# A first unit's projections in an order of their own, six gate tiles ahead of the convolution tiles, and a wider pad ahead of the scan's buffers

## The reference

```python
proj = input_states @ in_proj_w.T
gate, xBC, dt = proj[..., :8192], proj[..., 8192:18432], proj[..., 18432:]
xBC = silu(causal_conv4(xBC) + conv_b)
hs, Bm, Cm = xBC (128 heads of 64), 8 groups of 128, 8 groups of 128
dt = softplus(dt + dt_bias);  A = -exp(A_log);  cum = cumsum(dt * A)
y = scan over the sequence(hs, A, Bm, Cm, D, dt)
g = group_rms_norm(y * silu(gate)) * norm_w
x = x + g @ out_w.T                      # input_states = layernorm(x)
x = x + ffn(layernorm(x))                # ffn(x) = lin2(silu(lin1(x)) * lin3(x))
```

## Time and profile before

| | |
|---|---|
| median of 3 runs | 1926.45 us (1924.99 to 1927.78) |
| profiled execution, its own time | 1926.12 us |
| span in its profile | 1924.3 us |
| PE busy | 1817.4 us, 94% of the span |
| DVE busy | 1204.2 us, 63% |
| ACT busy | 1143.8 us, 59% |
| POOL busy | 1066.4 us, 55% |

### The profile page before, as it was taken

The page is one execution under the profiler, slowest core; times in us unless marked ns, Lnnn a source line. Parts: engine busy times, 40 slices in busy tenths (PEclk is TensorE's granted clock), DMA queues, the critical chain, the costliest instruction groups (busy, mean ns, idle before and its releaser), DMA issues.

```text
span 1924.3 us, 27364 instructions
## 1 busy us (share of the span) xinstructions
PE 1817.4 (94%) x9826; PEld 1448.3 (75%) x9826; DVE 1204.2 (63%) x2070; ACT 1143.8 (59%) x2185; POOL 1066.4 (55%) x989
## 2 busy tenths in 40 slices
PE   5879999999999999999999999999999997689999
PEld 3668777778777877787778777787777785467767
DVE  5456667766776768666867686668667776613112
ACT  4666667666766676666766676667666764322111
POOL 3346666666656566665756575757565654432121
PEclk9989999999999999999999999999999998889989
DMA  3523334333433343334433353335333522221001
GB/s 121 152 90 116 107 116 151 115 103 116 151 110 109 107 144 104 121 89 140 125 105 119 116 147 107 115 105 163 106 113 104 157 86 69 73 71 37 28 21 44
DMA packets 118709, 205.36 MB, mean 107 GB/s; under 512 B 23888, under 2 KB 28368, under 8 KB 118576
## 3 DMA queue, kind: packets, MB, share of 16 engines
q1 hardware_dynamic: 118576, 203.62, 34.8%
HBM read 198.85 MB, written 4.72 MB: 106 GB/s over the span
## 4 chain that ended last, share of the span: by engine, by line
PE 80%; DVE 10%; POOL 5%; ACT 2%; issue 2%; DMA 1%; SPq 0%; DVEq 0%; POOLq 0%; ACTq 0%
PE bank L1280 15%; PE bank L1282 14%; PE bank L1281 14%; PE bank L1343 6%; PE bank L1381 5%; PE bank L1356 5%; PE bank L1383 4%; PE bank L1382 4%; PE bank L1369 3%; PE bank L1321 3%; DVE ow_l L1074 2%; DVE x_ch L1068 2%; DVE bcT L1068 2%; POOL xw L614 1%; DVE xdt L1087 1%
## 5 line engine op out<-in xcount | busy, mean ns | idle before, releaser
L596 POOL TENSOR_TENSOR w_l<-w_raw,w_h 128x512 fp32r<-128x512 f32 x288 | 373.0, 1298 | 315.1 <-ACT w_h L726 313.7
L1280 PE MATMUL bank<-x_h,w_h 128*128 128x512 f32 x1160 | 473.5, 408 | 24.3 <-DVE bcT L1068 11.2
L1282 PE MATMUL bank<-x_h,w_l 128*128 128x512 f32 x1160 | 459.8, 396 | 0.0
L1281 PE MATMUL bank<-x_l,w_h 128*128 128x512 f32 x1160 | 459.6, 396 | 0.0
L1068 DVE SCALAR_TENSOR_TENSOR x_ch<-bank,par,x_ch 128x511 f32<-128x511 f32 (+2 forms) x384 | 287.3, 748 | 129.6 <-ACT x_ch L743 120.5
L774 ACT ACTIVATE decay<-decay,cols 128x128 f32<-128x128 f32 x1024 | 317.0, 390 | 0.7
L1280 PEld LDWEIGHTS bank<-x_h,w_h 128*128 128x128 f32 x1160 | 219.7, 189 | 88.0 <-issue 25.1
L1282 PEld LDWEIGHTS bank<-x_h,w_l 128*128 128x128 f32 x1160 | 219.7, 189 | 52.1
L602 POOL TENSOR_SCALAR_AFFINE_SELECT decay<-decay 128x512 f32<-128x512 f32 x256 | 199.8, 793 | 100.6 <-DMA decay<-cum_scratch 100.6
L1281 PEld LDWEIGHTS bank<-x_l,w_h 128*128 128x128 f32 x1160 | 220.3, 190 | 45.7
L1381 PE MATMUL bank<-ow_h,gT_h 128*128 128x512 f32 x512 | 226.3, 442 | 16.3 <-POOL gT_l L620 16.3
(11 more groups left out here) (135 smaller groups left out, 2853.5 us busy)
## 6 DMA issues: line engine op xcount, KB each, us to landing
w_raw<-in_wp SPq DMA_DIRECT2D x288, 256.0 KB, 3.4
decay<-cum_scratch SPq DMA_DIRECT2D x256, 256.0 KB, 4.0
ec<-ecum_scratch SPq DMA_DIRECT2D x96, 256.0 KB, 5.0
ow_raw<-in_ow SPq DMA_DIRECT2D x64, 256.0 KB, 4.8
raw<-in_w SPq DMA_DIRECT2D x20, 256.0 KB, 2.9
w_raw<-in_w SPq DMA_DIRECT2D x10, 256.0 KB, 3.5
acc<-in_x SPq DMA_DIRECT2D x8, 256.0 KB, 4.9
out<-acc SPq DMA_DIRECT2D x8, 256.0 KB, 2.0
```

The lines of the kernel that those rows point to most:

```text
L596: pool.tensor_tensor(w_l[:, s, :], w_raw[:, s, :], w_h[:, s, :].bitcast(F32), ALU.subtract).then_inc(wl_ready, 1)
L1280: pe.matmul(dst, wh, xh, start=(k == 0), stop=False)
L1281: pe.matmul(dst, wh, xl, start=False, stop=False)
L1282: last = pe.matmul(dst, wl, xh, start=False, stop=(k == len(terms) - 1 and not more))
```

## The change

- In the first unit the tiles go in the order `FIRST_ORDER`: g0 to g5, c0 to c9, g6, g7. All other units keep `TILE_ORDER`. SP picks the weights' places by it.
- On PE the transposes of the last two token tiles come behind the first step-size product, and the second step-size product comes behind the first tile.
- ACT reads the six early gates out with a plain copy, and applies the SiLU to all six at once (3,072 columns) behind the third convolution tile. `early_gates` tells DVE of it before the first gating. The exponentials of chunk 0 stand ahead of the readout of g6 and g7, with the copy of B (`copy_b`) behind the first four of them.
- The columns are turned after tiles 10, 11 and 12 (before: 8, 10, 12) and copied right there. SP's stores and refills are put in an order that follows.
- The first group's `ow_high` and `ow_low` are split and moved: four `ow_high` behind g7, four in chunk 0's body; all eight `ow_low` in chunk 0's body, where every other group has them.
- The pad has 448 bytes in place of 64, so every buffer of the scan lies 384 bytes higher.

The core of the diff:

```diff
+EARLY_GATES = 6
+FIRST_ORDER = [("g", t) for t in range(EARLY_GATES)] + [t for t in TILE_ORDER if t[0] == "c"] + [("g", 6), ("g", 7)]
-TURN_AT = (8, 10, 12)
-COLS_AT = (9, 11, 13)
+TURN_AT = (10, 11, 12)
...
-        sb("align", [P, 16])
+        sb("align", [P, 112])
...
@@ gate (ACT)
-                act.activation(sgT[:, bu, t, :], pj[i % 2][:, :], ACT.Silu).then_inc(gate_done, 1)
+                if u == 0 and t < EARLY_GATES:
+                    act.activation(sgT[:, bu, t, :], pj[i % 2][:, :], ACT.Copy).then_inc(gate_done, 1)
+                else:
+                    act.activation(sgT[:, bu, t, :], pj[i % 2][:, :], ACT.Silu).then_inc(gate_done, 1)
...
@@ ACT, first unit
+            for i in range(TILES - 2):
+                drain(0, 0, i)
+                w_high(0, (i + LEAD) // TILES, (i + LEAD) % TILES)
...
+                if i == EARLY_GATES:
+                    decayed(0)
+                if i == EARLY_GATES + 2:
+                    decayed(1)
...
+                    early = sgT[:, 0, 0:EARLY_GATES, :]
+                    act.activation(early, early, ACT.Silu).then_inc(early_gates, 1)
+                    silu(0, 0, [0, 1])
+                if i in TURN_AT:
+                    copy_cols(TURN_AT.index(i))
+                if i > EARLY_GATES + 2:
+                    silu(0, 0, [i - EARLY_GATES - 1])
+            silu(0, 0, [9])
+            for q in range(QUARTERS):
+                exps(0, 0, q)
+                if q == 0:
+                    copy_b(0, 0)
+            for i in range(TILES - 2, TILES):
                 drain(0, 0, i)
                 w_high(0, (i + LEAD) // TILES, (i + LEAD) % TILES)
...
-            for j in range(CT):
+            for j in range(OW_EARLY):
                 ow_high(0, j)
-            for q in range(QUARTERS):
-                exps(0, 0, q)
-            copy_b(0, 0)
...
@@ DVE
-            for j in range(CT):
-                ow_low(0, j)
             scale_x(0, 0)
...
-                    if k == 0 and some(g):
+                    if k == 0:
                         for j in range(OW_EARLY):
                             ow_low(g, j)
...
@@ PE
+            for c in range(CHUNKS - 2):
+                norm_transpose(0, c)
+            pe.wait_ge(wdt_l_ready, 1)
+            step_product(0)
+            for c in range(CHUNKS - 2, CHUNKS):
+                norm_transpose(0, c)
...
             for i in range(TILES):
                 project(0, 0, i)
+                if i == 0:
+                    step_product(1)
                 turn_cols(i)
```

More of the change, by code:

```diff
@@ L295, in build @@
         gate_done = sem("gate_done")
+        early_gates = sem("early_gates")
         tx_done = sem("tx_done")
@@ L466, in refill, with store_cols @@
                 load_w(0, (i + WRING) // TILES, (i + WRING) % TILES)
[L468 to L474, removed]
-            for q in range(QUARTERS):
[L476 to L491, removed]
+            def store_cols(k):
                 for b in range(BATCH):
@@ L502, in _ @@
             load_unit(0, 0)
-            for i in range(COLS_AT[-1] + 1, TILES):
+            load_ow(0, 0)
+            for i in range(TURN_AT[-1] + 2, TILES - 1):
                 refill(i)
+            sp.wait_ge(rows_stored, 16 * BATCH)
+            sp.wait_ge(ecum_stored, 32 * BATCH)
             def body(g, last):
@@ L810, in _, with copy_cols @@
[L810 to L817, removed]
+            def copy_cols(k):
+                for b in range(BATCH):
+                    m = k * BATCH + b
+                    act.wait_ge(cols_psum, m + 1)
+                    if m >= 4:
+                        act.wait_ge(cols_stored[m % 4], 16)
+                    src = xt[b][:, :].rearrange("p (c g h) -> p g c h", c=SC, g=GROUPS)
+                    dst = colsT[m % 4].rearrange("p (g c h) -> p g c h", g=GROUPS, c=SC)
+                    act.activation(dst, src, ACT.Copy).then_inc(cols_out, 1)
@@ new lines, in decayed @@
+            def decayed(b):
+                act.wait_ge(dve_head, head_last(b))
+                act.activation(ecumT[:, seq(b)], ncumT[:, seq(b)], ACT.Exp, scale=-1.0).then_inc(act_head, 1)
+                act.activation(elastT[:, seq(b)], fix[:, seq(b)], ACT.Exp).then_inc(act_head, 1)
+            act.wait_ge(small_loaded, 32)
+            absolute(0)
+            for i in range(1, LEAD):
+                w_high(0, 0, i)
+            for i in range(TILES - 2):
+                drain(0, 0, i)
+                w_high(0, (i + LEAD) // TILES, (i + LEAD) % TILES)
+                if i == 0:
+                    absolute(1)
+                    for b in range(BATCH):
+                        act.wait_ge(act_head, b + 1)
+                        act.activation(expz[:, seq(b)], absz[:, seq(b)], ACT.Exp, scale=-1.0).then_inc(act_head, 1)
+                    act.activation(a_pos[:, :], a_log[:, :], ACT.Exp).then_inc(act_head, 1)
@@ L818, in head @@
                 if i == 1:
+                    for b in range(BATCH):
+                        act.activation(sigz[:, seq(b)], absz[:, seq(b)], ACT.Sigmoid).then_inc(act_head, 1)
+                if i == 2:
                     act.wait_ge(act_head, act_sig(BATCH - 1))
@@ L831, in head @@
[L831 to L840, removed]
@@ L1395, in _, with step_product @@
             pe.wait_ge(const_ready, 1)
[L1396 to L1399, removed]
+            def step_product(b):
                 pe.wait_ge(x_l_ready, SC * (b + 1))
```

92 lines of the change are left out of this document (55 added, 37 removed).

## The result

The changed kernel takes **1891.5 us** (median of 4 runs, 1889.3 to 1893.4), the kernel before, run beside it on the same chip, 1926.8 (4 runs, 1925.0 to 1927.8). The ratio is 0.9817, with a 95% interval from 0.980 to 0.983. That is 35 us faster, where 21 were forecast, and outside the range given. The profiled execution of the changed kernel took 1893.4 us, its span is 1891.6.

The account below looks back on a forecast made before the run. PE bounds the kernel, busy 94% of the span, with some 41 us left in the first stage. Chunk 1's product moves from 145.9 to 124.5, 21.4 us: 1926.12 becomes 1904.7, with 0.33 for the median 1905 us; range 1896 to 1914.

Parts of the forecast that it names:

- the pad: Scan's buffers 384 bytes higher: no effect taken, with 2 ns on each of 4,992 matmuls, 10 us either way, as ends.
- Rival C: All matmuls of 512 columns: the pad makes each somewhat faster, 10 us at the 2 ns end, 1895 us; chance 0.10.
- Start: First stage up to g5: g0 starts at 25.1 after a wait near 1.9 us at full clock, otherwise 1.6 us later.
- Convolution tiles: c0 to c9, g6, g7: new 4.9 us wait ahead of c3, 1.6 us lost to low clock; this part gives 14.4 us.
- Chunk 0's product: End of the first stage: the product ends at 95.9 where before it was 120.5, gain so far 24.6 us.
- ACT's table loads: Path to the first chunk's product, twice: 1.28 us each with no extra drain; the skill's rule would add 1.4 us.
- Rest of chunk 0: From the first chunk's product's end to the second's start: 24.55 + 1.5 + 0.5 + 0.6 + 1.4 = 28.6 us.
- The other three terms of the sum: Inside chunk 0: g6's bank 0.5 us late, DVE's gating waiting for g7 0.6, low clock after the product's pieces 1.4.
- Queues: SP's stores and loads in the first unit: columns land at 80 against a need at 86.9, decay masked by 60; all hidden.
- Rival E: First stage: columns or masks come late behind SP's second sum store, chunk 0's product slides 10 us, 1915 us; chance 0.06.
- Rival B: Chunk 0 gives more back: ow_high's lateness passes to output product and second half, up to 6 us more, 1911; chance 0.17.
- rival D: PE's matmuls: the pad slows its reads; at 7 ns each 35 us are lost, 1940 us; chance 0.05.

Follow-up runs that it names:

- experiment 8: The changed kernel with all eight ow_high back ahead of the first exponentials and all eight ow_low ahead of the first scaling; 1894.7 us in one execution.
- experiment 1: The kernel before with the pad of 448 bytes and nothing else; 1912.1 us against 1925.2, ratio 0.9928.
- experiment 9: The changed kernel with only w_high(0) two token tiles earlier on ACT; 1891.1 us (1887.3 to 1894.1), ratio 0.9822.

## Why the prediction was wrong

**The step that failed is the pad.** It said "I take nothing, with 10 us of gain and 10 of loss as ends". It is worth 13.1 us by itself, beyond the end given: 4.6 ns on each projection matmul, not 2. The count was off as well: 3,480 matmuls gain on lines 1280 to 1282 ahead of the feed-forward, 16.0 us at 4.6 ns each, of which part is lost in the 7 chunks that DVE bounds; the 1,536 of the output product do not gain, since their operands stood at equal places before. The feed-forward, which the count left out, gives 2.5 us with the pad alone. Rival C, "the pad speeds the loop", named the right direction and what would show it in the profile (a distance other than 26.5) and had a chance of 0.10. With 13.1 us in place of its 10 it would have given 1905 - 13 = 1892.

Why the step went wrong: the evidence was from the wrong engine. An activation that writes a buffer on either side of the pad says nothing of how PE reads two buffers at once. The trace of before held a comparison that none of the rows shown had: projections at 232.6 ns, and beside them an output product at 229.3 and the feed-forward's second product at 227.5, all of one shape. That alone would not have named the pad, but "nothing in the rows speaks for it" holds only for the rows that were taken. The page's means, 396 ns and 395 to 397, hide the difference.

**The order was right.** The order alone is worth 18.8 us (interval some 3 to either side) where 21.4 were forecast. Step by step, against the profiled execution of that kernel, which is the fastest of its four:
- *Start.* g0 was to start at 25.1 after 1.9 us; it starts at 23.25 there and at 24.17 in the changed kernel, after 2.12 us. The full clock that was assumed holds in the first (its first matmul records 0.50) and not in the second (0.79, and the window from 24.1 shows 0.57). There the other end came: g0 took 4.38 us (24.17 to 28.55) in place of 2.8, the forecast 1.6 more.
- *Convolution tiles.* A wait of 4.9 us ahead of c3 was forecast and 5.8 to 5.9 came. head(1) was to take 5.3 us and took 6.6 (50.85 to 57.47). All that it grew by over the 4.9 us of before is in two of its steps, line 1081 (1.40 us for 0.49) and line 1088 (1.69 for 0.88), and POOL works beside both (52.83 to 54.13 and 55.46 to 56.88). The kernel before had shown it already: the same step took 1.37 us beside POOL (busy from 40.66 to 42.18) and 0.49 with POOL idle:

```profile
41.09 1.37 DVE L1049 TENSOR_SCALAR sgT<-x_ch,a_pos 128x512 f32<-128x512 f32 x1
...
49.08 0.49 DVE L1049 TENSOR_SCALAR sgT<-x_ch,a_pos 128x512 f32<-128x512 f32 x1
```

  and in the changed kernel:

```profile
50.85 0.68 DVE L1076 TENSOR_TENSOR sgT<-sgT 128x512 f32<-128x512 f32 x1
...
53.02 1.40 DVE L1081 TENSOR_SCALAR sgT<-x_ch,a_pos 128x512 f32<-128x512 f32 x1
...
57.47 2.31 DVE L1101 SCALAR_TENSOR_TENSOR bcT<-bank,par,bcT 128x511 f32<-128x511 f32 x3
```

  c3 started at 57.97 with the order alone and at 59.92 in the changed kernel; forecast 58.5. The low clock behind the wait came too (0.50 in the window from 59.9), and was priced too low: c3's twelve matmuls took 5.1 us with the order alone (57.97 to 63.10), 2.3 more than a tile at full clock, where 1.6 were added, though the prediction's own two readings were 1.8 and 2.4.
- *Chunk 0's product* was to end at 95.9. It ended at 96.2 with the order alone and at 98.5 in the changed kernel. Of the 2.6 us that the latter is late, 1.4 are there when c3 starts, and the rest comes behind it.
- *ACT's table loads.* No drain showed:

```profile
89.08 1.28 ACT L794 ACT_TABLE_LOAD   x1
90.38 1.28 ACT L794 ACTIVATE decay<-decay,cols 128x128 f32<-128x128 f32 x4
```

  89.08 + 1.28 = 90.36 and the next begins at 90.38; the activation ahead of the load ends at 89.07. The Trainium skill's extra 1.38 us ("ScalarE: Activation LUTs", "What ACT_TABLE_LOAD costs") would have been an error here.
- *Rest of chunk 0*: 28.6 us forecast, 28.3 with the order alone and 28.1 in the changed kernel (98.46 to 126.58). It is 1.8 us longer than in experiment 8, whose chunk 0 has no part of ow inside; the forecast had put 1.5 on ow_low. The other three terms of the sum were not tested one by one. An ow_low there took 1.45 us (5.78 for four), not the 1.3 named.
- *Queues*: the second sum's store went at 55.85 and the columns were loaded from 81.63, ahead of the first exponential at 90.38. Hidden, as forecast. Rival E did not occur.
- *Chunk 1's product*: forecast 124.5, with the order alone 124.47, in the changed kernel 126.58. The order alone took 1906.4 us against 1905 forecast. That the starts agree to 0.03 us is luck: g0 came 1.9 us early, the wait and the low clock took 1.6 more than forecast, and smaller errors made up the rest. One execution against another moves the start by 2 us.

Rival B (chunk 0 gives more back) fell by the 28.1 us; rival D (the pad slows PE) by experiment 1. The Trainium skill's rule on descriptors off a 256-byte boundary ("DMA: Bandwidth & Descriptors", "How a descriptor splits into AXI transactions") also had no effect that shows: loads of w_raw land in 3.4 us and of decay in 4.0 in both kernels, and with the pad alone in 3.5 and 3.9.

## What to carry to other kernels

When a layout edit is costed, look at the engine that reads the buffers, with rows of that engine, and compare start to start over many instructions, not the page's means. Where PE is busy for 95%, try the stationary and the moving operand at the same place within 256 bytes: here it cost one line and gave 13 us of 1925. And when one wait is cut, ask what has been standing in its shade: here, behind the split head, stood ACT with the SiLU of six gates, and the wait for it went from 3.50 to 0.20 us when that was split as well.

## What was not expected of the hardware

A matmul of 512 columns by a 128x128 weight of this type costs 227 to 229.6 ns from start to start when its two operands in SBUF start at the same place within 256 bytes, and 232.2 to 233.3 when they are 64 or 128 bytes apart. Equal places were tried at 0 and at 128 past a multiple, both fast. Three products were seen both ways, the projections, the output product and the feed-forward's product with x; a fourth never had its operands apart and never changed. Why it is so is not shown: neither the trace nor these runs say which access waits, and distances other than 0, 64 and 128 were not tried.

A DVE operation can take nearly three times as long beside a busy POOL: 1.37 and 1.40 us against 0.49 for a 128x512 multiplication.

Kernels with the same first stage differ by 2 us in it, by where the clock stands when the first products come: the first matmul of g0 records 0.50 us with the order alone and 0.79 in the changed kernel behind the same wait of 2.12 us, with the latter's window at 0.57. Executions of one kernel lie up to 6.8 us apart (experiment 9). A single execution's time therefore decides nothing below some 4 us here; distances between chunks, which repeat to some 0.03 us, do.
